# Guarded counts and negated means computed on GpSimd, with every queue ordered anew

## The reference

```
h = relu(layernorm(x));  L = D^-1/2 (A + I) D^-1/2;  x = x + L (h W + b)          # layer 0
h = relu(layernorm(x));  H = (adj != 0);  w = adj[first row]                       # layer 1
Dn = 1/(H w);  Be = 1/(column counts of H);  P = H Be H^T
h = relu(Dn * P (h W1^T) + b1);  h = layernorm(h) * gamma + beta                   # 1024 wide
x = x + Dn * P (h W2^T) + b2
```

## Time and profile before

| | us |
|---|---|
| median of 3 runs | 1919.46 (1917.72 to 1922.2) |
| the profiled execution | 1921.86 |
| its span, first to last instruction | 1920.0 |
| PE busy | 1871.1 |
| DVE busy | 1663.5 |
| ACT busy | 1451.3 |
| GpSimd busy | 1226.8 |

### The profile page before, as it was taken

The page is one execution under the profiler, slowest core; times in us unless marked ns, Lnnn a source line. Parts: engine busy times, 40 slices in busy tenths (PEclk is TensorE's granted clock), DMA queues, the critical chain, the costliest instruction groups (busy, mean ns, idle before and its releaser), DMA issues.

```text
span 1920.0 us, 37001 instructions
## 1 busy us (share of the span) xinstructions
PE 1871.1 (97%) x9926; PEld 896.1 (47%) x9926; DVE 1663.5 (87%) x3177; ACT 1451.3 (76%) x2726; POOL 1226.8 (64%) x1554
## 2 busy tenths in 40 slices
PE   5889999999999999999999999999999999999998
PEld 2344444444444444444444444444444444444443
DVE  6998988988988988989988988988889988888774
ACT  5788778778778778778778778778778778787664
POOL 4766766756766666666766766766666766576660
PEclk9899999999999999999999999999999999999999
DMA  8254554554554554453554554554554554544333
GB/s 230 56 102 93 110 112 89 108 110 92 106 113 91 107 111 92 109 112 91 108 112 91 108 109 94 108 112 92 108 111 92 109 108 95 110 93 98 83 67 78
DMA packets 518735, 197.64 MB, mean 103 GB/s; under 512 B 466816, under 2 KB 483328, under 8 KB 518528
## 3 DMA queue, kind: packets, MB, share of 16 engines
q1 hardware_dynamic: 518528, 195.27, 47.6%
HBM read 48.31 MB, written 33.55 MB: 43 GB/s over the span
## 4 chain that ended last, share of the span: by engine, by line
PE 77%; issue 7%; DVE 6%; POOL 4%; DMA 3%; SPq 1%; ACT 1%; DVEq 0%; POOLq 0%; ACTq 0%
PE ps_u L405 28%; PE ps_e L405 14%; PE ps_x L416 14%; PE ps_z L416 7%; PE ps_y L416 3%; DMA raw_t<-bet_wide 2%; PE ps_y L456 1%; PE ps_y L458 1%; PE ps_y L457 1%; PE ps_t L393 1%; PE ps_t L395 1%; PE ps_t L394 1%; PE ps_e L456 1%; PE ps_e L458 1%; PE ps_e L457 1%
## 5 line engine op out<-in xcount | busy, mean ns | idle before, releaser
L405 PE MATMUL ps_u<-w2h,raw_t 128*128 128x512 f16 x2016 | 477.8, 380 | 0.0
L1488 POOL TENSOR_TENSOR base<-b_all,xh 128x512 f32<-128x512 f32 x128 | 210.4, 1644 | 366.3 <-DVE raw_w L1123 356.3
L405 PEld LDWEIGHTS ps_u<-w2h,raw_t 128*128 128x128 f16 x2016 | 195.0, 98 | 225.2 <-issue 2.8
L1065 DVE SCALAR_TENSOR_TENSOR raw_w<-ps_x,dn,b_all 128x512 f32<-128x512 f32 x192 | 141.8, 739 | 117.5 <-PE ps_x L416 117.0
L405 PE MATMUL ps_u<-w2l,raw_t 128*128 128x512 f16 x1008 | 238.1, 379 | 0.0
L770 ACT ACTIVATE bet_wide<-raw_w 128x1024 f16<-128x1024 f32 x128 | 134.2, 1048 | 77.3 <-DMA raw_t<-bet_wide 73.5
L1480 POOL TENSOR_TENSOR b_all<-x,b_all 128x512 f32<-128x512 f32 x128 | 166.9, 1304 | 15.5 <-DMA b_all<-in_b_dram 6.4
L1493 POOL TENSOR_TENSOR base<-base,raw_w 128x512 f32<-128x512 f32 x128 | 166.8, 1303 | 8.0
L1538 POOL TENSOR_SCALAR u<-ssq 128x2 f32<-128x2 f32 x64 | 31.7, 496 | 216.4 <-ACT raw_w L755 215.8
L1109 DVE TENSOR_TENSOR bet_wide<-raw_w,bet_wide 128x1024 f16<-128x1024 f32 x128 | 158.9, 1242 | 8.0 <-DMA raw_t<-bet_wide 4.3
L761 ACT ACTIVATE raw_w<-raw_w,nm,sc 128x1024 f32<-128x1024 f32 x128 | 151.9, 1232 | 18.4 <-POOL nm L1564 18.2
(11 more groups left out here) (174 smaller groups left out, 4860.7 us busy)
## 6 DMA issues: line engine op xcount, KB each, us to landing
x_t<-in_x_dram SPq DMA_DIRECT2D x128, 256.0 KB, 2.9
out_dram<-raw_w SPq DMA_DIRECT2D x128, 256.0 KB, 2.5
adj_t<-in_adj_dram SPq DMA_DIRECT2D x64, 128.0 KB, 2.1
raw_t<-bet_wide SPq DMA_TRANSPOSE x256, 3.3
...
h0T_hi<-h_hi SPq DMA_TRANSPOSE x128, 2.5
h0T_lo<-h_lo SPq DMA_TRANSPOSE x128, 2.4
...
```

Of the source, the lines that this page charges most:

```text
L405: mm = pe.matmul(ps, t[:, j * 128:(j + 1) * 128], w[:, j, :], start=(n == 0 and j == 0), stop=(n == 2 and j == blocks - 1))
L1065: return dve.scalar_tensor_tensor(out=z, in0=bank[:, :], scalar=dn1[:, p % 2, j:j + 1], in1=z if row is None else row[:, cols], op0=ALU.mu ...
L1488: pool.tensor_tensor(base[:, g % 6, :], x1b[:, :], xh[:, g % 2, :], ALU.add).then_inc(s_scr2, 1)
```

## The change

cm and nmu leave the vector queue for the GpSimd queue, with the same waits, the same arithmetic and the same signals:

```diff
@@ vector
-            def do_cm(p):
-                m = p % 2
-                dve.wait_ge(s_cnt, 2 * p + 2)
-                dve.tensor_scalar(cm[:, m, :], cnt[:, m, :], 1.0, 1.0 / P_SCALE, ALU.max, ALU.mult).then_inc(s_cm, 1)
-            def do_nmu(p):
-                dve.wait_ge(s_h, 2 * p + 2)
-                done(dve, s_sq, 2 * p - 2)
-                done(dve, s_ln2, p - 1)
-                dve.tensor_scalar(nmu[:, p % 2, :], hsum[:, p % 2, :], -1.0 / DH, None, ALU.mult).then_inc(s_nmu, 1)
@@ gpsimd
+            def do_cm(p):
+                m = p % 2
+                pool.wait_ge(s_cnt, 2 * p + 2)
+                pool.tensor_scalar(cm[:, m, :], cnt[:, m, :], 1.0, 1.0 / P_SCALE, ALU.max, ALU.mult).then_inc(s_cm, 1)
+            def do_nmu(p):
+                pool.wait_ge(s_h, 2 * p + 2)
+                done(pool, s_sq, 2 * p - 2)
+                done(pool, s_ln2, p - 1)
+                pool.tensor_scalar(nmu[:, p % 2, :], hsum[:, p % 2, :], -1.0 / DH, None, ALU.mult).then_inc(s_nmu, 1)
```

All five queues have a new order with the same instructions otherwise. The start is written out up to pair 13, and the loop runs over k from 14 to 47:

```diff
-    STEADY_FROM, STEADY_TO = 4, NP - 16
+    STEADY_FROM, STEADY_TO = 14, NP - 16
@@ tensor, the start as far as U(0)
-            do_Z0(0); do_P(1); do_Z0(1); do_Y0(2)
+            do_Z0(0); do_P(1); do_Z0(1)
+            beta_row(range(0, 2))
             weight_sum(2, wsq[:, 0:KH])
-            do_Y0(3); do_Z0(2)
-            beta_row(range(0, 2))
-            do_T1(0); do_Z0(3)
+            do_Y0(2); do_Y0(3)
             beta_row(range(2, 4))
             beta_row(range(4, 6))
-            do_P(2); do_T1(1)
+            do_P(2)
             beta_row(range(6, 8))
-            do_Y0(4); do_M1(0); do_Z0(4); do_M2(0); do_M5(0); do_Y0(5); do_M6(0); do_M3(0); do_T1(2); do_M7(0)
-            do_Z0(5); do_T1(3); do_M4(0); do_Y0(6); do_M1(1); do_P(3); do_M2(1); do_Z0(6); do_M6(1); do_Y0(7)
-            do_M5(1); do_M3(1); do_M7(1); do_Z0(7); do_M4(1); do_Y0(8); do_T1(4); do_T1(5); do_Z0(8); do_U(0)
+            do_Z0(2); do_Z0(3); do_Y0(4); do_T1(0); do_T1(1); do_Z0(4); do_Y0(5); do_M1(0); do_M2(0); do_T1(2)
+            do_M6(0); do_M5(0); do_M7(0); do_M3(0); do_Z0(5); do_P(3); do_T1(3); do_M4(0); do_Y0(6); do_M2(1)
+            do_M1(1); do_M5(1); do_M6(1); do_Z0(6); do_M3(1); do_Y0(7); do_P(4); do_M7(1); do_T1(4); do_M4(1)
+            do_T1(5); do_U(0); do_M1(2); do_Z0(7); do_U(1); do_Y2(0); do_Y0(8); do_M6(2); do_M5(2); do_M7(2)
@@ tensor, the loop
-                do_M1(k); do_Y0(2 * k + 5); do_U(2 * k - 3); do_M6(k); do_Y2(2 * k - 4); do_P(k+2); do_T1(2 * k + 2)
-                do_M7(k); do_Z0(2 * k + 5); do_M5(k); do_Y0(2 * k + 6); do_Y2(2 * k - 3); do_M3(k); do_M4(k)
-                do_M2(k); do_T1(2 * k + 3); do_U(2 * k - 2); do_Z0(2 * k + 6)
+                do_M1(k); do_Z0(2 * k + 6); do_T1(2 * k + 2); do_U(2 * k - 3); do_Y0(2 * k + 7); do_M6(k)
+                do_Y2(2 * k - 4); do_M5(k); do_M7(k); do_M3(k); do_Y2(2 * k - 3); do_Z0(2 * k + 7); do_M2(k)
+                do_Y0(2 * k + 8); do_P(k+3); do_M4(k); do_T1(2 * k + 3); do_U(2 * k - 2)
@@ scalar, the loop
+                do_uh(2 * k - 4); do_sq(2 * k - 1); do_thS(k); do_h0_hi(2 * k + 8); do_h0_hi(2 * k + 9)
+                do_h0(2 * k + 8); do_h0(2 * k + 9); do_tf(2 * k + 2); do_hn(2 * k - 2); do_hn(2 * k - 1)
+                do_uh(2 * k - 3); do_hn_hi(2 * k - 2); do_yh(2 * k + 7); do_P_hi(2 * k + 4); do_hn_hi(2 * k - 1)
+                do_xh(2 * k + 4); do_P_hi(2 * k + 5); do_xh(2 * k + 5); do_h(2 * k); do_vq(2 * k + 4)
+                do_yh(2 * k + 8); do_vq(2 * k + 5); do_cntH(2 * k + 10); do_tf(2 * k + 3); do_cntH(2 * k + 11)
+                do_thA(k+1); do_xh_hi(k+2); do_h(2 * k + 1); do_rsum(2 * k + 16); do_rsum(2 * k + 17); do_A_hi(k+8)
+                do_sq(2 * k)
@@ vector, the loop
+                do_inv(k+4); do_A_lo(k+7); do_ul(2 * k - 4); do_z1(k); do_x1(2 * k + 6); do_tlS(k)
+                do_st1(2 * k + 6); do_HB_hi(2 * k + 8); do_HB_hi(2 * k + 9); do_ahat(k+8); do_HB_lo(2 * k + 8)
+                do_h0_lo(2 * k + 8); do_HB_lo(2 * k + 9); do_bn0(2 * k + 10); do_h0_lo(2 * k + 9)
+                do_aggr0(2 * k + 10); do_aggr1(2 * k + 6); do_ul(2 * k - 3); do_hn_lo(2 * k - 2); do_yv(2 * k + 7)
+                do_z6(k); do_out(2 * k - 4); do_yl(2 * k + 7); do_z5(k); do_z7(k); do_z3(k); do_out(2 * k - 3)
+                do_dm(k+2); do_x1(2 * k + 7); do_ri(k+2); do_P_lo(k+2); do_st1(2 * k + 7); do_z2(k); do_dn(k+2)
+                do_aggr1(2 * k + 7); do_hn_lo(2 * k - 1); do_yv(2 * k + 8); do_bn0(2 * k + 11); do_aggr0(2 * k + 11)
+                do_z4(k); do_u0(k+5); do_yl(2 * k + 8); do_w(k+5); do_dds(k+7); do_tlA(k+1); do_xh_lo(k+2)
+                do_Hu(k+8)
@@ gpsimd, the loop
+                do_cm(k+4); do_S2(k); do_S4(k); do_bias0(2 * k + 8); do_bias0(2 * k + 9); do_u2(k-1); do_sc2(k-1)
+                do_nm2(k-1); do_scr2(2 * k + 2); do_x1b(2 * k + 3); do_base2(2 * k + 2); do_scr2(2 * k + 3)
+                do_base2(2 * k + 3); do_qdn(k+2); do_u1(k+3); do_x1b(2 * k + 4); do_dn2(k+2); do_sc1(k+3)
+                do_rd0(k+5); do_dn1(k+2); do_nm1(2 * k + 6); do_S3(k+1); do_nm1(2 * k + 7); do_nmu(k); do_cx(k+5)
+                do_S1(k+1)
```

More of the change, by code:

```diff
@@ L352, in _ @@
[L352 to L361, removed]
@@ new lines, in _ @@
+            do_ldX(33); do_trh(22); do_trl(22); do_ldA(22); do_trh(23); do_tr0h(32); do_trl(23); do_st(20)
+            do_ldX(34); do_tr0l(32); do_tr0h(33); do_st(21); do_tr0l(33); do_trA(18); do_ldX(35); do_ldA(23)
+            do_trh(24); do_trl(24); do_tr0h(34); do_st(22); do_ldX(36); do_st(23); do_trh(25); do_tr0h(35)
+            do_trl(25); do_trA(19); do_ldX(37); do_tr0l(34); do_tr0l(35)
+            for k in range(STEADY_FROM, STEADY_TO):
+                do_ldA(k+10); do_ldX(2 * k + 10); do_tr0h(2 * k + 8); do_tr0l(2 * k + 8); do_trh(2 * k - 2)
+                do_tr0h(2 * k + 9); do_tr0l(2 * k + 9); do_st(2 * k - 4); do_trl(2 * k - 2); do_trh(2 * k - 1)
+                do_st(2 * k - 3); do_ldX(2 * k + 11); do_trl(2 * k - 1); do_trA(k+6)
@@ new lines, in _ @@
+            do_U(NG - 35); do_M7(NP - 16); do_Y2(NG - 36); do_M5(NP - 16); do_Z0(NG - 25); do_T1(NG - 29)
+            do_Y2(NG - 35); do_M3(NP - 16); do_M4(NP - 16); do_U(NG - 34); do_Y0(NG - 24); do_M1(NP - 15)
+            do_P(NP - 13); do_U(NG - 33); do_M6(NP - 15); do_Z0(NG - 24); do_Y2(NG - 34); do_M7(NP - 15)
+            do_Y0(NG - 23); do_T1(NG - 28); do_Y2(NG - 33); do_M5(NP - 15); do_M2(NP - 15); do_T1(NG - 27)
+            do_M3(NP - 15); do_P(NP - 12); do_M4(NP - 15); do_Z0(NG - 23); do_U(NG - 32); do_Y0(NG - 22)
@@ new lines, in _ @@
+            do_Y2(NG - 29); do_M3(NP - 13); do_M4(NP - 13); do_Y0(NG - 18); do_P(NP - 10); do_U(NG - 28)
+            do_M1(NP - 12); do_Z0(NG - 18); do_T1(NG - 22); do_M6(NP - 12); do_Y0(NG - 17); do_M7(NP - 12)
+            do_U(NG - 27); do_Y2(NG - 28); do_M5(NP - 12); do_Z0(NG - 17); do_Y2(NG - 27); do_M3(NP - 12)
+            do_M2(NP - 12); do_M4(NP - 12); do_Y0(NG - 16); do_P(NP - 9); do_T1(NG - 21); do_U(NG - 26)
+            do_M1(NP - 11); do_Z0(NG - 16); do_T1(NG - 20); do_U(NG - 25); do_Y0(NG - 15); do_M6(NP - 11)
@@ new lines, in _ @@
+            do_Y2(NG - 26); do_M5(NP - 11); do_M7(NP - 11); do_M3(NP - 11); do_Y2(NG - 25); do_Z0(NG - 15)
+            do_M2(NP - 11); do_Y0(NG - 14); do_P(NP - 8); do_M4(NP - 11); do_T1(NG - 19); do_U(NG - 24)
+            do_M1(NP - 10); do_Z0(NG - 14); do_T1(NG - 18); do_M2(NP - 10); do_Y0(NG - 13); do_M6(NP - 10)
+            do_U(NG - 23); do_M7(NP - 10); do_Y2(NG - 24); do_M5(NP - 10); do_Z0(NG - 13); do_T1(NG - 17)
+            do_Y2(NG - 23); do_M3(NP - 10); do_M4(NP - 10); do_U(NG - 22); do_Y0(NG - 12); do_M1(NP - 9)
@@ new lines, in _ @@
+            do_M4(NP - 8); do_Z0(NG - 9); do_P(NP - 5); do_U(NG - 18); do_Y0(NG - 8); do_M1(NP - 7); do_U(NG - 17)
+            do_M6(NP - 7); do_Y2(NG - 18); do_Z0(NG - 8); do_T1(NG - 12); do_M5(NP - 7); do_M7(NP - 7)
+            do_Y0(NG - 7); do_M3(NP - 7); do_Y2(NG - 17); do_M2(NP - 7); do_M4(NP - 7); do_Z0(NG - 7)
+            do_T1(NG - 11); do_U(NG - 16); do_Y0(NG - 6); do_M1(NP - 6); do_U(NG - 15); do_M6(NP - 6)
+            do_Y2(NG - 16); do_T1(NG - 10); do_M7(NP - 6); do_Y2(NG - 15); do_M5(NP - 6); do_Z0(NG - 6)
@@ new lines, in _ @@
+            do_vq(NG - 4); do_vq(NG - 3); do_thS(NP - 3); do_yh(NG - 1); do_hn(NG - 8); do_hn(NG - 7)
+            do_hn_hi(NG - 8); do_uh(NG - 9); do_P_hi(NG - 2); do_tf(NG - 4); do_hn_hi(NG - 7); do_tf(NG - 3)
+            do_P_hi(NG - 1); do_vq(NG - 2); do_thS(NP - 2); do_thA(NP - 2); do_vq(NG - 1); do_h(NG - 6)
+            do_h(NG - 5); do_xh(NG - 2); do_xh(NG - 1); do_uh(NG - 8); do_xh_hi(NP - 1); do_sq(NG - 6)
+            do_sq(NG - 5); do_hn(NG - 6); do_uh(NG - 7); do_hn_hi(NG - 6); do_tf(NG - 2); do_hn(NG - 5)
@@ L919, in _ @@
+            do_hn_hi(NG - 5); do_h(NG - 4); do_tf(NG - 1); do_h(NG - 3); do_thA(NP - 1); do_sq(NG - 4)
+            do_sq(NG - 3); do_thS(NP - 1); do_uh(NG - 6); do_hn(NG - 4); do_hn(NG - 3); do_hn_hi(NG - 4)
```

(36 more changed lines are left out.)

987 lines of the change are left out of this document (533 added, 454 removed).

## The result

The changed kernel takes 1942.15 us (median of 4 runs, 1941.35 to 1945.13), the kernel before 1920.75 in the same comparison: a ratio of 1.0119, 95% interval 1.0107 to 1.0131. Slower by 21 us. The forecast was 1923.8 with a range to 1933: the side was right, the size missed by a factor of five. The profiled execution took 1942.78 us, its span 1940.9.

A forecast was written before the change was run, and what follows sets the result against it. PE was taken to bound the loop. Start -1.5 and loop +5.8 gave +4.3 us on the profiled 1921.86, so 1926.2, or 1923.8 as median; own range 1923 to 1929, over the cases 1912 to 1933.

The forecast's parts named there:

- Bound: In the loop PE is full at 28.76 us a pair; the change can gain only in the start, lose anywhere.
- What counts is their place: Loop: cm and nmu, moved to GpSimd, matter by queue place; 0.2 to 1.1 us of slack, cost taken as 0.
- the way by ul: Loop: from T1(2k+3) by tf, h, nmu, cm, inv, A_lo, ul to U(2k-3); 6.7 to 7.6 us against 7.8.
- the ring: Loop: tf to hn_hi on ACT, hn_lo to z5 on DVE, M3 to T1 on PE; 29.2 us against 28.76.
- The mis-sized term: Loop: the pair becomes 0.17 us slower (bounds 0 and 0.5), over 34 turns +5.8 us (0 to 17).
- Rival C: Loop: nmu and cm slow behind a held port, U(2k-3) late; 0.4 us a pair in all, 14 us, 1932; chance 0.08.
- The start: Up to the first U and M1: less DVE work ahead, a gain of 1.5 us (bounds 2.7 and -1.2).
- The end: After the loop: same work in another order, +-1 us, taken as 0.

The follow-up runs named there:

- Experiment 2: The changed kernel with nmu put back on VectorE in the loop's 34 turns, cm staying on GpSimd: 1931.45 us, ratio 1.0065.
- experiment 3: The changed kernel with z5(k) put ahead of yl(2k+7) on VectorE in the loop: 1939.09 us, ratio 1.0111.

## Why the prediction missed

- **Bound.** Right: PE has nothing to give in the loop, the change could lose anywhere.
- **"What counts is their place ... 0.2 to 1.1 us of slack, and I take 0 for it."** This step failed. I put nmu at 0.26 us directly behind h. It stands behind nm1(2k+7), which ends only after xh_lo, so it is done 1.27 us after h instead of 0.26. I had seen that "xh_lo can hold nmu(k) back by some tenths", but counted only the instruction itself as held, not the one ahead of it, and checked only the way by ul. sq waits for nmu too, and sq is in the ring of the next step. Experiment 2 prices it: 0.36 us a pair, 12 us over 34 turns by the period, 10.4 by the two ratios.
- **The ring.** 29.2 summed, 29.22 measured, and the agreement is luck. The ACT stretch was summed at 15.61 us, all work; it took 15.28 of work and 0.40 of waiting for nmu, so one error hid the other. And between out and tf the ring does not run over yl, z5, M3 and T1, as the sum has it, but over GpSimd's queue, qdn and vq: 10.31 us, where the way through TensorE takes 10.19 by the same rows (1.26 for yl and z5, 0.05, 8.62 from M3 to T1's last matmul, 0.26). The prediction saw that yh and vq stand ahead of tf, up to 0.1 late; it did not follow them back to GpSimd.
- **The mis-sized term.** "I take 0.17, under the middle, since my sum's parts are all at their full cost". 0.46 was the truth, 15.6 us for 34 turns instead of 5.8 (14 net of the x1 waits that the kernel before had). The discount itself did little harm: with nmu in time the loop has 0.10 over 28.76 (experiment 2). What 0.17 lacks is the 0.36 of the nmu step.
- **Rival C** named the mechanism (nmu behind a held port) and nearly its size (0.4 a pair, 14 us), but sent it by cm and A_lo to U alone. That way is there, 0.13 us ahead of U(2k-3) in the changed kernel and 0.37 in experiment 3; the longer one is nmu's to sq, inside the ACT stretch of the forecast's own sum. The rival should have been a term of the ring, and not another case at 0.08.
- **The start.** -1.5 was taken; nothing to be seen, inside the bounds.
- **Pairs 4 to 13** had no term. The start was counted to the first U and the loop from pair 14 on, and ten written-out pairs in between, in an order that I had not walked through, cost 6 us by the account of lost time. A second failed step; why they cost it is open.
- **The end.** 3 us by the account against 1 allowed; no experiment confirms it.
